# Queries of the next batch scaled and split on VectorE during attention, a sixteenth per head

## The reference, cut to what matters

```python
q = (x @ Wq.T + bq).reshape(B, L, H, hd).transpose(0, 2, 1, 3)
k = (x @ Wk.T + bk).reshape(B, L, H, hd).transpose(0, 2, 1, 3)
sim = jnp.einsum('bhid,bhjd->bhij', q, k) / jnp.sqrt(jnp.asarray(hd, x.dtype))
sim = sim / temp
for fi, freq in enumerate(FREQS):
    scores = scores + a * jnp.sin(TWO_PI * sim / freq + p)
w = jax.nn.sigmoid(scores)
w = w / (jnp.sum(w, axis=-1, keepdims=True) + 1e-10)
out = jnp.einsum('bhij,bhjd->bhid', w, v)
```

## Time and profile before

| what | us |
|---|---|
| median of 3 runs | 7122.15 (7116.23 to 7126.51) |
| the profiled execution's own time | 7119.98 |
| its span | 7118.2 |
| projection | 0 to 412.6 |
| set-up of attention | 412.6 to 473.2 |
| attention | 473.2 to about 6213 |
| last block | to 7118.2 |
| busy: PE, DVE, ACT | 6113.5, 5773.2, 5853.0 |

### The profile page before, as it was taken

The page is one execution under the profiler, slowest core; times in us unless marked ns, Lnnn a source line. Parts: engine busy times, 40 slices in busy tenths (PEclk is TensorE's granted clock), DMA queues, the critical chain, the costliest instruction groups (busy, mean ns, idle before and its releaser), DMA issues. The chain is left out here.

```text
span 7118.2 us, 130314 instructions
## 1 busy us (share of the span) xinstructions
PE 6113.5 (86%) x48057; PEld 4363.9 (61%) x48057; DVE 5773.2 (81%) x4353; ACT 5853.0 (82%) x5874; POOL 205.8 (3%) x217
## 2 busy tenths in 40 slices
PE   6539999999999999999999999999999999826555
PEld 3326666666666666666666666666666666625444
DVE  6648888888888888888888888888888888857775
ACT  1139999999999999999999999999999999901111
POOL 0000000000000000000000000000000000010000
PEclk8769999999999999999999999999999999966666
DMA  7931111111111111111111111111111111131220
GB/s 291 358 143 47 47 47 46 46 47 46 45 47 45 45 47 47 47 46 47 46 47 46 47 47 46 47 45 46 47 45 46 47 45 47 30 81 46 50 52 20
DMA packets 322961, 446.10 MB, mean 63 GB/s; under 512 B 158980, under 2 KB 189604, under 8 KB 321384
## 3 DMA queue, kind: packets, MB, share of 16 engines
q1 hardware_dynamic: 317032, 432.81, 19.4%
q0 software_dynamic: 5376, 5.30, 0.3%
HBM read 284.11 MB, written 153.75 MB: 62 GB/s over the span
## 5 line engine op out<-in xcount | busy, mean ns | idle before, releaser
L593 ACT ACTIVATE a_wave<-a_ps_turn 128x1024 f32<-128x1024 f32 x5120 | 4915.0, 1365 | 132.2 <-PE a_ps_turn L527 131.9
L527 PE MATMUL a_ps_turn<-a_q_r,a_k_r 64*128 64x512 f32 x20480 | 3392.0, 399 | 399.8 <-ACT a_wave L593 249.3
L609 DVE SCALAR_TENSOR_TENSOR a_weight<-a_wave,a_head_c,a_weight 128x2048 f32<-128x2048 f32 x1536 | 3612.6, 2352 | 59.5
L527 PE MATMUL a_ps_turn<-a_q_r,a_rounder 64*128 64x512 f32 x20480 | 3241.4, 392 | 4.6 <-issue 4.6
L527 PEld LDWEIGHTS a_ps_turn<-a_q_r,a_k_r 64*128 64x128 f32 x20480 | 1951.8, 185 | 1574.9 <-ACT a_wave L593 804.5
L527 PEld LDWEIGHTS a_ps_turn<-a_q_r,a_rounder 64*128 64x128 f32 x20480 | 1976.6, 186 | 244.6 <-issue 9.4
L609 DVE SCALAR_TENSOR_TENSOR a_weight<-a_wave,a_head_c 128x2048 f32<-128x2048 f32 x512 | 1203.9, 2351 | 844.4 <-ACT a_wave L593 844.4
L587 ACT ACTIVATE a_weight<-a_weight,a_head_c 128x2048 f32<-128x2048 f32 x512 | 1186.0, 2316 | 5.2 <-DVE a_weight L609 5.2
L547 PE MATMUL a_ps_out<-a_weight,a_v_r 128*32 128x512 f32 x4096 | 547.2, 606 | 7.6 <-ACT a_weight L587 5.4
L506 POOL COPY a_head_c<-a_table 128x5 f32 (+1 forms) x128 | 114.3, 893 | 5596.2 <-ACT a_weight L587 5596.1
L547 PEld LDWEIGHTS a_ps_out<-a_weight,a_v_r 128*32 128x32 f32 x4096 | 80.8, 108 | 194.7 <-issue 184.0
(11 more groups left out here) (231 smaller groups left out, 1919.3 us busy)
## 6 DMA issues: line engine op xcount, KB each, us to landing
q_d<-p_q_hl SPq DMA_DIRECT2D x80, 1024.0 KB, 8.3
a_q_r<-q_d SPq DMA_DIRECT2D x256, 320.0 KB
a_k_r<-k_d SPq DMA_DIRECT2D x512, 128.0 KB
a_q_r<-q_d SPq DMA_DIRECT2D x256, 160.0 KB
k_d<-p_k_hl SPq DMA_DIRECT2D x8, 4096.0 KB, 15.2
a_k_r<-k_d SPq DMA_DIRECT2D x512, 64.0 KB
o_d<-a_out SPq DMA_DIRECT2D x512, 34.0 KB
num<-o_d SPq DMA_DIRECT2D x32, 512.0 KB
```

The lines of the kernel that those rows point to most:

```text
L527: last = nc.tensor.matmul(ps_turn[slot_of(r, s, f)][:, half, :], exact(w(rows[half])), exact(q_r[rows[half], k, f, :]), start=(i == 0), st ...
L593: nc.scalar.activation(wave[:, s // 2 % 2, f, s % 2, :], ps_turn[slot_of(r, s, f)][:].rearrange("p a b -> p (a b)"), ACT.Sin, scale=TURN_I ...
L609: return v.scalar_tensor_tensor(both(weight[:, i, :, :]), both(wave[:, i % 2, f, :, :]), head_c[:, k, f:f + 1], to, ALU.mult, ALU.add)
```

## The change

The projection scales and splits the queries of batch 0 only, into a new DRAM tensor `qs_d`; of every batch it keeps the unsplit queries in `q_d` (1 MB). In attention, each head (b, j) of batches 0 to 6 also processes one sixteenth of the queries of batch b + 1: SP fetches 128 x 128 numbers one head ahead (`fetch_q`), VectorE makes 128 x 640 products, their rounded form and the rest (`split_q`, three instructions, between pair 0 and pair 1), and SP writes the two results to `qs_d` (`keep_q`), ahead of `load` of the next head. At the end of a batch SP waits until these writes have landed. VectorE and SP loop over batches with 16 heads written out, instead of over pairs of heads.

```diff
@@ -126,20 +126,24 @@
...
                     sp.sem_inc(q_kept[f], 16)
+                sp.sem_inc(whole_kept, 16)
                 sp.sem_inc(k_kept, 16)
...
-                def keep(b):
+                def keep(b, split=False):
+                    sp.wait_ge(q_ready, b + 1)
+                    sp.dma_start(q_d[b, :, :].rearrange("(m p) l -> p m l", p=P), qk_sb[:, 0, :, :]).then_inc(whole_kept, 16)
                     sp.wait_ge(v_ready, b + 2)
                     sp.dma_start(v_d[b, :, :, :], v_sb[:]).then_inc(v_kept, 16)
-                    for m in range(KC):
-                        for f in range(NF):
-                            sp.wait_ge(q_split, NF * (KC * b + m) + f + 1)
-                            sp.dma_start(q_d[b, :, m * P:(m + 1) * P, f, :].rearrange("i p l -> p i l"),
-                                         q_hl[:, f, :, :]).then_inc(q_kept[f], 16)
+                    if split:
+                        for m in range(KC):
+                            for f in range(NF):
+                                sp.wait_ge(q_split, NF * m + f + 1)
+                                sp.dma_start(qs_d[b, :, m * P:(m + 1) * P, f, :].rearrange("i p l -> p i l"),
+                                             q_hl[:, f, :, :]).then_inc(q_kept[f], 16)
                     sp.wait_ge(k_split, b + 2)
...
...
@@ -151,7 +155,11 @@
...
                     sp.dma_start(rate[:, m, :], tab_d[8 * m:8 * m + 8, 1, :].unsqueeze(1).broadcast_to([8, HD, NF])).then_inc(rate_in, 16)
-                with sp.Fori(0, B // 2 - 1, 1) as pair:
+                for b in range(2):
+                    sp.wait_ge(x_turned, b + 2)
+                    load(b + 2, b)
+                    keep(b, b == 0)
+                with sp.Fori(1, B // 2 - 1, 1) as pair:
                     for k in range(2):
...
...
@@ -288,20 +297,22 @@
...
-                def split_q(b, m):
+                def split_q(m):
...
                     for f in range(NF):
-                        dve.wait_ge(q_kept[f], 16 * (KC * b + m + 1))
+                        dve.wait_ge(q_kept[f], 16 * (m + 1))
                         nc.vector.tensor_scalar(q_hl[:, f, 0, :].bitcast(F32R), whole, rate[:, m, f:f + 1], None,
...
                     for f in range(NF):
-                        dve.wait_ge(q_step, NF * (KC * b + m) + f + 1)
+                        dve.wait_ge(q_step, NF * m + f + 1)
                         nc.vector.scalar_tensor_tensor(q_hl[:, f, 1, :].bitcast(F32R), whole, rate[:, m, f:f + 1],
...
-                with dve.Fori(0, B, 1) as b:
+                def body(b, split):
                     dve.wait_ge(q_summed, b + 1)
+                    dve.wait_ge(whole_kept, 16 * (b + 1))
                     for m in range(KC):
...
...
@@ -309,9 +320,10 @@
...
                                             AX.X, ALU.add).then_inc(x_summed, 1)
-                    dve.wait_ge(q_ready, b + 1)
-                    dve.wait_ge(rate_in, 32)
-                    split_q(b, 0)
+                    if split:
+                        dve.wait_ge(q_ready, b + 1)
+                        dve.wait_ge(rate_in, 32)
+                        split_q(0)
                     dve.wait_ge(v_summed, b + 2)
...
...
@@ -319,7 +331,6 @@
...
                     last.then_inc(v_ready, 1)
-                    split_q(b, 1)
                     dve.wait_ge(k_ready, b + 2)
...
...
@@ -329,6 +340,12 @@
...
                     nc.vector.tensor_scalar(part(2, 4).bitcast(F32R), part(0, 2), -1.0, None, ALU.mult).then_inc(k_split, 1)
+                    if split:
+                        split_q(1)
+                        dve.wait_ge(q_split, NF * KC)
+                body(0, True)
+                with dve.Fori(1, B, 1) as b:
+                    body(b, False)
                 dve.wait_ge(totals, 1)
...
...
@@ -374,6 +392,10 @@
...
         v_r = sb("a_v_r", [P, 2, LT, VP])
+        q_in = sb("a_q_in", [P, 2, QW])
+        q_all = sb("a_q_all", [P, NF, QW])
+        q_hl = sb("a_q_hl", [P, 2, 2, NF, QW])
+        rate = sb("a_rate", [P, KC, NF])
         warm = sb("a_warm", [P, 2])
...
...
@@ -410,6 +434,17 @@
...
+        def heads_by_batch(eng, body):
+            for j in range(H):
+                body(0, j)
+            with eng.Fori(1, B - 1, 1) as b:
+                for j in range(H):
+                    body(b, j)
+            for j in range(H):
+                body(B - 1, j)
+            body(B, 0)
...
...
@@ -445,38 +480,67 @@
...
-                def load(g, k):
+                for m in range(KC):
+                    sp.dma_start(rate[:, m, :], tab_d[8 * m:8 * m + 8, 1, :].unsqueeze(1).broadcast_to([8, HD, NF])).then_inc(rate_in, 16)
+                def load(b, j):
+                    g, k = H * b + j, j % 2
                     wait_pos(sp, filled, NF * U * (g - 1))
-                    b, h = g // H, g % H
                     to_q = lambda row, count, src: sp.dma_start(q_r[row:row + count, k, :, :], src).then_inc(qk_loaded[k], 16)
                     to_k = lambda row, count, i, src: sp.dma_start(k_r[row:row + count, k, i, :], src).then_inc(qk_loaded[k], 16)
-                    dims, head = bass.ds(h * HD, HD), bass.ds(h, 1)
-                    for j in range(2):
+                    dims = slice(j * HD, (j + 1) * HD)
+                    for n in range(2):
                         for i in range(2):
-                            to_k(64 * j, 2 * HD, i, k_d[b, 2 * i:2 * i + 2, dims, :])
-                            to_k(64 * j + 2 * HD, HD, i, k_d[b, 2 * i, dims, :])
-                        to_q(64 * j, 2 * HD, q_d[b, 0:1, dims, :, halved(j)].broadcast_to([2, HD, NF, HALF]))
-                        to_q(64 * j + 2 * HD, HD, q_d[b, 1, dims, :, halved(j)])
-                        to_q(64 * j + 3 * HD, 2, ph_d[:, head, :, halved(j)].rearrange("i o f l -> i (o f) l"))
+                            to_k(64 * n, 2 * HD, i, k_d[b, 2 * i:2 * i + 2, dims, :])
+                            to_k(64 * n + 2 * HD, HD, i, k_d[b, 2 * i, dims, :])
+                        to_q(64 * n, 2 * HD, qs_d[b, 0:1, dims, :, halved(n)].broadcast_to([2, HD, NF, HALF]))
+                        to_q(64 * n + 2 * HD, HD, qs_d[b, 1, dims, :, halved(n)])
+                        to_q(64 * n + 3 * HD, 2, ph_d[:, j:j + 1, :, halved(n)].rearrange("i o f l -> i (o f) l"))
...
-                def store(g, k):
+                part_of = lambda j: (slice(j // 8 * P, (j // 8 + 1) * P), slice(j % 8 * QW, (j % 8 + 1) * QW))
+                def fetch_q(b, j):
+                    wait_pos(sp, q_split, H * b + j - 1)
+                    dims, cols = part_of(j)
+                    sp.dma_start(q_in[:, j % 2, :], q_d[b + 1, dims, cols]).then_inc(q_loaded[j % 2], 16)
+                def keep_q(b, j):
+                    sp.wait_ge(q_split, H * b + j + 1)
+                    dims, cols = part_of(j)
+                    for i in range(2):
+                        sp.dma_start(qs_d[b + 1, i, dims, :, cols], q_hl[:, j % 2, i, :, :]).then_inc(q_kept[j % 2], 16)
+                def store(b, j):
+                    g, k = H * b + j, j % 2
                     sp.wait_ge(out_ready, g)
                     for c in range(4):
-                        sp.dma_start(o_d[(g - 1) // H, c // 2, bass.ds((g - 1) % H, 1), :, halved(c % 2)].rearrange("o c l -> (o c) l"),
+                        sp.dma_start(o_d[b if j else b - 1, c // 2, (j - 1) % H, :, halved(c % 2)],
                                      out[VP * c:VP * c + VW, 1 - k, :]).then_inc(stored[1 - k], 16)
...
-                def body(g, k):
-                    if not isinstance(g, int) or g + 1 < HEADS:
-                        load(g + 1, 1 - k)
-                    if after(g):
-                        store(g, k)
-                heads_of(sp, body)
+                def body(b, j):
+                    ahead = not isinstance(b, int) or b < B - 1
+                    if ahead:
+                        if j == 0:
+                            fetch_q(b, 0)
+                        if j < H - 1:
+                            fetch_q(b, j + 1)
+                        keep_q(b, j)
+                        if j == H - 1:
+                            for k in range(2):
+                                sp.wait_ge(q_kept[k], 16 * H * (b + 1))
+                    if ahead or b == B - 1 and j < H - 1:
+                        load(b + (j + 1) // H, (j + 1) % H)
+                    if not isinstance(b, int) or b or j:
+                        store(b, j)
+                heads_by_batch(sp, body)
                 for k in range(2):
...
...
@@ -609,8 +674,23 @@
...
-                def body(g, k):
+                def split_q(b, j):
+                    g, k = H * b + j, j % 2
+                    dve.wait_ge(q_loaded[k], 8 * H * b + 16 * (j // 2 + 1))
+                    wait_pos(dve, q_kept[k], 16 * H * b + 32 * (j // 2))
+                    v.tensor_tensor(q_all[:], q_in[:, k, :].unsqueeze(1).broadcast_to([P, NF, QW]),
```

(32 more changed lines are left out.)

## The result

The changed kernel takes 8489.5 us (median of 4 runs, 8479.5 to 8493.5) against 7120.8 us for the kernel before in the same session: a ratio of 1.192, 95% interval 1.190 to 1.194. The forecast was 8580 us, with a range of 8200 to 8850. So the time is inside the range, and 90 us under the forecast.

A forecast was written before the change was run, and what follows sets the result against it. DMAs were taken to bound the projection and ScalarE attention. From 7120 us: projection -138.6, set-up +1.4, late heads +1534, stops in code +40, batch ends +21, giving 8578 (forecast 8580), range 8200 to 8850 us.

The forecast's parts named there:

- The mechanism: SP in attention: the next head's loads (32.1 us) wait behind the running head's split, making heads 1 to 112 late.
- The signs asked for: Attention trace: heads about 58 us apart, some 12 us first-fill wait released by a load, one clock drop per head.
- Loads that stay hidden: Rival, attention loads: they land within some 21 us of issue, only the projection counts, 6983 us; chance 4%.
- the last block: Code after attention: no term in the forecast, so counted as 0 us of change.
- each head takes 54.4 us: Rival, late heads: TensorE keeps full clock over 12 us stops and writes cost nothing, 8119 us in all; chance 17%.
- Dear writes: Rival, SP's small writes ahead of the loads: 6.5 us per head, heads of 63.5 us, 9138 in all; chance 12%.
- part of the loads slipping ahead: Rival, SP's queue: some loads pass the wait, heads late by a few us only, 7100 to 8000 us; chance 5%.
- The projection: First stage: splits and writes of batches 1 to 7 removed, ending at 274.0 instead of 412.6 us, gain 138.6 us.
- the late heads: Heads 1 to 112 of attention: 1534 us for spacing, plus 40 for stops in code and 21 for batch ends.
- the 58.5: Late head, one start to the next: 21.3 us to pair 0's sums, split 2.2, SP 1.4, loads 32.1, writes 1.5.
- The other four steps: Late head: first fill to first sum 11.6 us, pair 0's sums 9.7, split 2.2, SP's waking and issue 1.4.
- the stops in code and batch ends: Attention: stops partly showing again, 40 us, and SP waiting for writes at seven batch ends, 21 us.

The follow-up runs named there:

- The first two experiments: Changed kernel with the next head's loads ahead of SP's split wait and writes: 7018.0 us; changed kernel with the split before pair 0's sums: 7052.9 us.
- the third: Changed kernel with each load of leading dimension 2 issued as two loads of 16 rows, 20 per head instead of 14: 6995.1 us, ratio 0.983.
- the longer split: Changed kernel with the split's first product made four times, three more VectorE instructions of 0.82 us per head: 8713.3 us.

## Why the prediction was right, and where it was off

**The mechanism** was that of the text: SP's queue takes its instructions in order, behind the wait for the split stand the loads, and 32 us of loads are too long for what is left of a head. The first two experiments show the place on the queue, the third the length, and the longer split that each microsecond ahead of the loads counts. The signs asked for are there: a spacing of 57.9 us where some 58 was named, a wait of some 12 us ahead of each first fill, released by a load, the clock of 0.50 behind it, and the first load 1.9 us behind the split's end (1.5 was named).

**The rivals.** Loads that stay hidden (6983 us) came out only once they were spread or moved: 7018 and 6995 us, or 6983 and 6960 without the 35 of the last block. That each head takes 54.4 us needed the full clock, and it was 0.50. Dear writes needed 6.5 us; they are 1.3 with their issue. Against part of the loads slipping ahead stands the order of SP's rows in the late head.

**The projection** came out at -142.3 against -138.6, and step by step as forecast. The v products of batch 1 begin at 73.4 (72.8 was forecast) and the last ones end at 249.5 (250.8). The write of k took 12.4 us (257.90 to 270.31) instead of 14.9. These two, 1.3 and 2.5 us, are the difference.

**The term that was mis-sized** is the one of the late heads, 1595 against 1463, a miss of 132 us. The settled late head is 57.4 in the row and 57.55 in the median, 0.95 under the 58.5: the 33.6 us for loads with writes ahead were 32.65 in the median, because the writes' data cost 0.6 and not 1.5. The other four steps are off by 0.1 to 0.5 us each (the waking and issue of SP took 1.9 and not 1.4) and cancel. That is 112 x 0.95 = 106 us. Another 8 are the mean of the heads before, 44.87 over these 112 and not 44.8. The other 18 are the stops in code and batch ends: the mean stands 0.38 over the median, 43 us over 112 heads, where 61 were put down. That a late head hides part of such a stop, as TensorE waits for loads in any case, is an explanation that no run tested.

**What failed in the sum** is a term it did not have. The last block stood in it at nothing, without a reason, and took 34.7 us more. By luck this covers part of the overestimate: without it the forecast would have been 133 us too high and not 98 by the spans, still inside the range.

**The better kernel.** The projection's gain is real and is kept by either cure. The quickest of all was the changed kernel with spread loads and the loop of the last block in its good place: 6959.6 us, 2.2% under the kernel before, of which about 142 us come from the projection and 15 from the shorter loads of the first head (its first sine at 319.4, 335.1 in the changed kernel).

## What to carry to other kernels

A wait put on an in-order queue delays all that stands behind it: before moving work "off" a queue's path, list what the queue holds next and compare its slack with the transfers' whole length, from first issue to landing, and not with their issue. An engine that idles for 0.29 of the time can still be on the path for every microsecond, if a queue waits for it. If a load's leading dimension is 2, try splitting it before anything is put in front of it: here that halved 32 us and made the order harmless.

## What the runs showed of the hardware that was not expected

- A stop of 3 to 5 us per turn of a loop on VectorE that comes or goes with 64 one-column instructions in front of it: 96.3 to 101.3 us a turn in the kernel before, 101.2 to 96.6 in the spread one, some 35 us of 7120, or 0.5% either way. Whoever compares two versions at this level measures that too.
- Fourteen loads, six of them with a leading 2 (the two small ones of the phases apart), took 32.1 us. With these six made into twelve with a leading 16, for the same bytes, it was 16.9 us, and the DMA share went from 0.13 in the slice of the earlier trace rows to 0.33 to 0.95 in the four slices shown. SP's issuing fell from 21.3 to 10.3 us, though there were more to issue.
- Behind a stop of TensorE of 11.8 us the first 5 us had a granted clock of 0.50 (1.2 GHz), and the next 5 us 0.98; that was worth 2.35 us of a head, measured by keeping it busy.
